# Attention loop: three PSUM banks taken by age for chunks, maxima and turns, P·V in one bank, and the score pair first in a unit

## The chip, the core and the metric

The kernel runs on one core of one Trainium2 chip. The metric is the device time of one execution in microseconds (us). Five engines run their own instruction streams and meet only at semaphores: TensorE (PE), VectorE (DVE), ScalarE (ACT), GpSimd (POOL) and SyncE (SP), which issues most of the DMAs. PE writes its products to PSUM, which has eight banks of 128 x 512 float32.

## What is computed

Attention over 4 batches of 1024 tokens with 16 heads of 16 channels, with a residual and layer norms, and then a layer of 8 experts of which each token takes 2. The softmax is taken over all keys, and the causal mask is applied afterwards without a new normalisation.

```
x = L0_attn_content                                   # 4 x 1024 x 256
x = x + _layernorm(attn(_layernorm(x), Wq, Wk, Wv))
x = x + _layernorm(ffn(_layernorm(x), router_w, w_fc, w_proj))
# attn
scores = einsum('bqhd,bkhd->bhqk', Q, K) / sqrt(HEAD_DIM)
alpha = softmax(scores); alpha = where(causal, alpha, 0)
Y = einsum('bhqk,bkhd->bqhd', alpha, V)
# ffn
topk_w, topk_idx = top_k(softmax(x @ router_w), 2)    # weights normalised
out = sum over e of combine[:, e] * (gelu(x @ w_fc[e]) @ w_proj[e])
```

## The kernel before

**Stages.** First the layer norm, Q, K and V of all tokens (up to about 150 us, already mixed with the first units of attention), then the attention loop (up to about 983 us), in whose last part the router and the first expert tile are worked in, and then 71 tiles of tokens through the experts. Only the attention loop is changed, with the two places where the experts begin.

**The loop.** The 64 pairs of batch and head are taken in 16 groups of four heads. A period is `U` = 32 units; period p works on the score pairs of group p, and on later steps of the groups before it. Every engine has its own `body`, which walks the same units in order. The order of steps inside a unit is as written there, and the unit of each step comes from the `at_...` lists: `due(at, k)` gives what stands in unit k, with how many periods back its group is. The steps of a group, counted in units from its first score pair:

- unit k, 0 to 31, **score pair**: two matmuls of 96 x 512 into banks 0 and 1 (k even) or 2 and 3 (k odd), line 1261. DVE reduces the 1024 scores of each query to a **maximum**, line 1699. Pair k waits until the maximum of k-2 is done.
- after every 8 units POOL splits the maxima into three bfloat16 parts (lines 731 to 737), PE transposes them (`at_m`, line 1274), ACT copies the result (line 905), and POOL spreads it into the last rows of the query operand (line 744).
- from unit 41, two **chunks** a unit, 64 in all: scores again, with the maximum taken off by the operand's last rows. Three of four are transposed scores (keys on partitions, line 1074), of which ACT takes the exponential into `et_sb` (line 921). The fourth, a corner (line 1067), is there for its row sum alone (line 916). The chunks go by turns to banks 4 and 5 (`ebank`), so a chunk waits for the exponential of the chunk two before; the last group has a ring of four.
- 12 **P·V bursts** (`pieces`, line 1104) at units 45, 48, 50, 53, 56, 58, 61, 64 for queries 512 to 1023 (bank 7), and 66, 69, 72, 74 for queries 0 to 511 (bank 6). A burst is 512 columns of float32 for four heads, each on its own 32 partitions; 8 of 12 have a diagonal part of 128 columns more, which waits for the mask product on POOL (line 765).
- `at_poc`, units 65 and 75: DVE **copies** the product out of its bank to `po_sb` (line 1710). `at_turn`, 67 and 77: PE **turns** it by four transposes back into the same bank (line 1248). `at_norm`, 69 and 79: DVE divides by the row sums (**norm**, lines 1720 to 1730). A burst on a bank's first key block waits for the norm of the group before.

The transposed maxima go to banks 6 and 7, rows 96 to 119, and wait for the norm there.

From period 6 on DVE and POOL also work on the layer norms of finished tokens (`steady`, `STEADY`, lines 1527 to 1558), in fixed units. In periods 16 and 17, the **tail**, no pairs are left, and the router's steps stand in their place.

**Order in a unit before.** PE: turn, P·V burst, first chunk, score pair, transpose of the maxima, second chunk. DVE: maximum reduction, layer norm step, copy, norm. ACT: copy of the maxima, then the exponentials.

## Time and profile before

| | |
|---|---|
| median of 3 executions | 1539.58 us (1539.1 to 1542.72) |
| profiled execution | 1539.73 us, of which its span is 1537.8 us |
| mean granted clock of PE in it | 0.983 of full speed |
| busy, share of the span | PE 92%, PE's weight loads 53%, DVE 60%, ACT 52%, POOL 40% |
| costliest group of DVE | line 1699, 512 maximum reductions, 607.2 us, 1217 ns each |
| costliest group of ACT | line 921, 768 exponentials, 436.1 us |
| attention loop on PE | chunks (lines 1067, 1074), pairs (1261) and bursts (1104) |

A matmul's row runs from its start to its modelled end and overlaps the next ones, so how long PE needs is read from start to start. "Idle before" names what an engine waited for. The window view gives busy times of each engine in a stretch.

### The profile page before, as it was taken

The page shows a single profiled execution, that of the slowest core. Times are in us where ns is not written, and L with a number is a line of the kernel's source. Part 1 is how long each engine was busy: PE and PEld are TensorE (multiplying, and loading weights), DVE is VectorE, ACT ScalarE, POOL GpSimd, SP SyncE. Part 2 cuts the span into 40 slices and gives each one's busy share as a digit, 9 for nine tenths or more (in the row PEclk, how much of TensorE's full clock was granted, in tenths as well). Part 3 has the DMA queues.
Part 4 walks back from the last instruction along what each step waited for, and adds up shares of the span by engine and source line. Part 5 has one row for each costly group of instructions (what it writes and reads, how often), then busy time and mean ns, then how long its engine had stood idle before and what let it go on. Part 6 is the DMA issues. An engine that isn't in the chain of part 4 may idle for free.

```text
span 1537.8 us, 28642 instructions
## 1 busy us (share of the span) xinstructions
PE 1417.4 (92%) x9774; PEld 820.1 (53%) x9775; DVE 925.1 (60%) x1740; ACT 805.4 (52%) x1717; POOL 610.9 (40%) x729
## 2 busy tenths in 40 slices
PE   6788999999999999999999998899999999999990
PEld 3444233333333233323332333699999999999980
DVE  4587787777888988898889887861111111111115
ACT  4444777777777777777777787321111111111114
POOL 2234334443454445444544441433333333333325
PEclk9999999999999999999999999999999999999995
DMA  3665732022202331223114141656666666666646
GB/s 122 155 158 126 247 42 42 7 37 42 42 15 28 42 42 18 25 42 42 20 23 97 56 138 57 175 163 192 172 178 191 176 178 187 182 175 182 189 113 222
DMA packets 100405, 166.85 MB, mean 108 GB/s; under 512 B 12400, under 2 KB 67568, under 8 KB 100304
## 3 DMA queue, kind: packets, MB, share of 16 engines
q1 hardware_dynamic: 86192, 146.08, 35.8%
q0 software_dynamic: 13632, 18.69, 7.6%
q10 hardware_dynamic: 480, 0.79, 0.3%
q8 instruction: 56, 0.92, 0.3%
q14 instruction: 45, 0.37, 0.1%
HBM read 130.76 MB, written 34.77 MB: 108 GB/s over the span
## 4 chain that ended last, share of the span: by engine, by line
PE 68%; DVE 18%; issue 6%; ACT 5%; POOL 2%; DMA 2%; ACTq 0%; POOLq 0%; DVEq 0%
PE ps L1206 16%; PE ps L1220 15%; PE ps L1104 11%; DVE negmax L1699 10%; PE ps L1074 9%; PE ps L1261 8%; ACT wfc L921 2%; PE ps L1043 2%; PE ps L1067 2%; POOL wfc L833 1%; PE ps L1248 1%; DVE x L1517 1%; PE ps L1193 1%; DVE mv L1506 1%; PE ps L1052 1%
## 5 line engine op out<-in xcount | busy, mean ns | idle before, releaser
L1699 DVE TENSOR_REDUCE negmax<-ps 128x1 f32<-128x1024 f32 x512 | 607.2, 1217 | 134.3 <-PE ps L1261 132.8
L921 ACT ACTIVATE wfc<-ps 128x512 f32<-128x512 f32 x768 | 436.1, 595 | 162.7 <-PE ps L1074 157.0
L976 ACT ACTIVATE wfc<-ps 128x512 f32<-128x512 f32 x142 | 84.8, 597 | 420.9 <-PE ps L1206 420.9
L1206 PEld LDWEIGHTS ps<-yx,wfc 128*128 128x128 f32 x2272 | 264.3, 192 | 4.2 <-issue 0.9
L1206 PE MATMUL ps<-yx,wfc 128*128 128x128 f32 x2272 | 265.7, 275 | 0.2 <-issue 0.2
L765 POOL TENSOR_TENSOR wfc<-wfc,causal 128x512 f32<-128x512 f32 x128 | 162.3, 1268 | 241.3 <-issue 108.8
L1220 PE MATMUL ps<-arena,wfc 128*128 x1136 | 257.3, 379 | 0.9 <-DMA arena<-in_L_ffn_w_proj 0.7
L821 POOL DMA_INDIRECT expert_out<-wfc,rt x71 | 113.0, 1592 | 299.9 <-DVE wfc L1663 291.9
L1220 PEld LDWEIGHTS ps<-arena,wfc 128*128 128x128 f32 x1136 | 210.3, 190 | 27.2 <-issue 1.6
L1261 PE MATMUL ps<-arena 96*128 96x512 bf16 x704 | 211.6, 382 | 9.1 <-DMA arena<-qk_parts 5.7
L1074 PE MATMUL ps<-arena 120*128 120x512 bf16 x528 | 202.0, 390 | 11.9 <-ACT wfc L921 0.4
L1104 PE MATMUL ps<-wfc 128*16 128x128 f32 (+4 forms) x2304 | 161.4, 381 | 0.1
L1663 DVE TENSOR_SCALAR wfc<-ps,rt 128x256 f32<-128x256 f32 x71 | 34.3, 483 | 203.1 <-PE ps L1220 203.1
L916 ACT ACTIVATE ps<-ps 128x512 f32<-128x512 f32 x256 | 149.6, 584 | 10.7 <-PE ps L1067 1.0
L1074 PEld LDWEIGHTS ps<-arena 120*128 120x128 bf16 x528 | 50.1, 96 | 183.9 <-ACT wfc L921 117.3
L1651 DVE SCALAR_TENSOR_TENSOR rt<-yx,rt 128x1 f32 (+1 forms) x71 | 15.5, 219 | 200.0 <-PE ps L1193 200.0
L1261 PEld LDWEIGHTS ps<-arena 96*128 96x128 bf16 x704 | 67.8, 99 | 63.1 <-issue 12.0
L1104 PEld LDWEIGHTS ps<-wfc 128*17 128x17 f32 (+1 forms) x2304 | 60.8, 97 | 75.2 <-issue 47.9
L1074 PE MATMUL ps<-wfc 120*128 120x512 bf16 x240 | 93.0, 388 | 6.4 <-ACT wfc L921 0.8
L1261 PE MATMUL ps<-wfc 96*128 96x512 bf16 x320 | 95.6, 379 | 0.3
L1104 PE MATMUL ps<-wfc,vone 128*17 128x128 f32 (+3 forms) x1024 | 94.6, 441 | 1.0
L744 POOL TENSOR_TENSOR arena<-mT,dmask 24x1024 bf16<-24x1024 bf16 x44 | 83.3, 1894 | 14.8 <-ACT mT L905 11.8
(208 smaller groups left out, 1259.3 us busy)
## 6 DMA issues: line engine op xcount, KB each, us to landing
wfc<-in_L_ffn_w_fc SPq DMA_DIRECT2D x71, 1024.0 KB, 5.3
arena<-qk_parts SPq DMA_DIRECT2D x126, 128.0 KB, 5.6
qk_parts<-x SPq DMA_DIRECT2D x32, 384.0 KB, 2.8
arena<-in_L_ffn_w_proj SPq DMA_DIRECT2D x8, 1024.0 KB, 8.3
wfc<-qk_parts SPq DMA_DIRECT2D x60, 128.0 KB, 5.8
expert_out<-rt SPq DMA_DIRECT2D x3, 1408.0 KB, 12.2
yx<-in_L_attn_content SPq DMA_DIRECT2D x8, 512.0 KB, 4.3
x<-in_L_attn_content SPq DMA_DIRECT2D x1, 4096.0 KB, 14.0
```

The lines of the kernel that those rows point to most:

```text
L744: pool.tensor_tensor(qs[(u - back) % NSL][MROW:MROW + MR, hl, :] .rearrange("p (i q) -> p i q", i=QT), mT[MROW:MROW + MR, :].unsqueeze(1). ...
L765: pool.tensor_tensor(md_sb[b % NET], et_sb[b % NET][:, :, q:q + P], causal[:, :].unsqueeze(1).to_broadcast([P, GH, P]), ALU.mult).then_inc ...
L821: pool.indirect_dma_start(out=ys_d, in_=yslot[t % 2], in_offset=None, out_offset=bass.IndirectOffsetOnAxis(ap=tok[:, t:t + 1], axis=0), co ...
L916: nc.scalar.activation(bk(ebank(c, g)), bk(ebank(c, g)), ACT.Exp, accum_out=den_u[:, (u - back) % NSL, hl, i:i + 1]).then_inc(s_expB, 1)
L921: nc.scalar.activation(et_sb[b % NET][:, hl, :], bk(ebank(c, g)), ACT.Exp).then_inc(s_expB, 1)
L976: nc.scalar.activation(hidT[s][:, 4 * hf:4 * hf + 4, :], bk(1 + hf).rearrange("p (c t) -> p c t", c=4), ACT.Gelu).then_inc(s_ge, 1)
L1074: nc.tensor.matmul(bk(ebank(c, g)), ks[v][0:MROW + MR, hl, i * P:(i + 1) * P], qs[v][0:MROW + MR, hl, hf * 512:(hf + 1) * 512], start=True ...
L1104: ins = nc.tensor.matmul(out[32 * hl:32 * hl + rows, q0:q1], lhs, rhs, start=(i == 0 and piece == 0 and n == 0), stop=False, skip_group_ch ...
L1206: ins = nc.tensor.matmul(bk(1 + hf)[:, c * P:(c + 1) * P], w1[s][:, kc * FF + (4 * hf + c) * P:kc * FF + (4 * hf + c + 1) * P], xsT[:, kc, :],
L1220: ins = nc.tensor.matmul(bk(5 + s)[:, 0:D], hidT[s][:, c, :], arena[:, ds(off + c * D, D)], start=(c == 0), stop=(c == FC - 1))
L1261: ins = nc.tensor.matmul(bk(2 * (k % 2) + hf), qs[u][0:SROWS, hl, i * P:(i + 1) * P], ks[u][0:SROWS, hl, hf * 512:(hf + 1) * 512], start=T ...
L1699: nc.vector.tensor_reduce(negmax[:, hl % 2, i:i + 1], ps[:, 2 * (k % 2):2 * (k % 2) + 2, :], AX.XY, ALU.max, negate=True).then_inc(s_max, 1)
```

## The change

Four things are changed, all in the attention loop.

1. **Banks.** Banks 4, 5 and 6 form one ring. A list of all its users in order (`ring_entries`: turns, chunks, maxima) is built, and each takes the bank whose last user is oldest (`ring_banks`). A turn's bank is not taken again by the next `HOLD` = 4 users. Each user waits for its bank's last one by name (`ring_free`): an exponential, a norm or a copy of maxima. The last group's ring of four goes. The first group's maxima stay in bank 7.
2. **P·V in bank 7 alone.** The first burst of each half waits for the copy of the half before it (`s_poc`), no longer for a norm.
3. **DVE.** Copy and norm stand ahead of the maximum reduction in their unit, and `at_norm` is two units earlier: the norm stands in the unit of its turn, 67 and 77.
4. **PE.** The score pair stands ahead of the burst and of both chunks.

In the tail the first tokens for the experts are transposed in bank 2 and no longer wait for a norm; the waits for the last exponential and the norm move from `first_half` and `transpose_x` to the first `second_half`.

```diff
-        at_norm = [x + 2 for x in at_turn]
+        at_norm = list(at_turn)
...
-        LAST_RING = (4, 5, 1, 2)
-
-        def ebank(c, g):
-
-            if isinstance(g, int) and g == NGR - 1:
-                return LAST_RING[c % 4]
-            return 4 + c % 2
...
+        def tx_bank(t):
+
+            return 2 if isinstance(t, int) and t == 0 else 7
...
+        def ring_entries():
+
+            out = []
+            for x in range(PRO, (NGR + 2) * U):
+                p, k = divmod(x, U)
+                out += [("turn", p - back, j) for j, back in due(at_turn, k) if live(p, back)]
+                chunks = [("chunk", p - back, c) for c, back in due(at_chunk, k) if live(p, back)]
+                out += chunks[:1]
+                out += [("maxima", p - back, hl) for hl, back in due(at_m, k) if live(p, back)]
+                out += chunks[1:]
+            return out
+
+        RING = ring_entries()
+        HOLD = 4
+
+        def ring_banks():
+
+            bank, user = {}, {}
+            last, held, until = {4: -3, 5: -2, 6: -1}, 0, -1
+            for n, x in enumerate(RING):
+                b = min((b for b in last if b != held or n > until), key=last.get)
+                bank[x], user[x] = b, RING[last[b]] if last[b] >= 0 else None
+                last[b] = n
+                if x[0] == "turn":
+                    held, until = b, n + HOLD
...
+            def ring_free(kind, g, x):
+                if RING_USER[kind, g, x] is None:
+                    return
+                last, g, x = RING_USER[kind, g, x]
+                if last == "chunk":
+                    pe.wait_ge(s_expB, NCH * g + x + 1)
+                elif last == "turn":
+                    pe.wait_ge(s_norm, 2 * g + x + 1)
+                else:
+                    pe.wait_ge(s_mtc, GH * g + x + 1)
+
             def chunk(p, u, c, back):
...
-                if isinstance(g, int) and g == NGR - 1 and c >= 2:
-                    pe.wait_ge(*((s_max, QT * NH) if c < 4 else (s_expB, NCH * g + c - 3)))
-                else:
-                    wait_pos(pe, s_expB, NCH * g + c - 1)
+                ring_free("chunk", g, c)
...
-                    et, out = et_sb[b % NET], bk(6 + hf)
+                    et, out = et_sb[b % NET], bk(7)
...
-                        wait_pos(pe, s_norm, 2 * (g - 1) + (j + 1))
-                        pe.wait_ge(s_mtc, min(GH * g + M_BEFORE_PV[j], NH) if isinstance(g, int) else
-                                   GH * g + M_BEFORE_PV[j])
+                        wait_pos(pe, s_poc, 2 * g + j)
...
             def first_half(t, s, hf):
-                if isinstance(t, int) and t == 0 and hf == 0:
-                    pe.wait_ge(s_expB, NCH * NGR)
...
                         pe.wait_ge(s_poc, 2 * (p - back) + (j + 1))
+                        ring_free("turn", p - back, j)
...
-                    pieces(p, u, k)
-                    todo = due(at_chunk, k)
-                    chunk(p, u, *todo[0])
                     if live(p, 0):
                         hl, i = divmod(k, QT)
...
                         ins.then_inc(s_S, 1)
+                    pieces(p, u, k)
+                    todo = due(at_chunk, k)
+                    chunk(p, u, *todo[0])
```

On DVE the blocks of the copy and of the norm move ahead of the block of the maximum reduction and of `steady`; ACT's exponentials only take the bank's new name.

The order on PE in units 65 to 67 of a later group, before: `s_expB` is the exponentials, `s_max` the maximum reductions, `s_sp` the split maxima, `s_poc` the copies. The first burst on queries 0 to 511 is the row with 17x128.

```order
L1261 MATMUL ps<-arena 128x512
L1274 MATMUL ps<-identb,mparts 24x128 [waits s_norm,s_sp]
L1074 MATMUL ps<-wfc 128x512 [waits s_expB]
L1104 MATMUL ps<-wfc,vone 17x128 [waits s_expB,s_mtc,s_norm]
...
L1261 MATMUL ps<-arena 128x512 [waits s_max]
L1261 MATMUL ps<-arena 128x512
L1067 MATMUL ps<-wfc 128x512 [waits s_expB]
L1248 MATMUL ps<-ident,wfc 128x128 [waits s_poc]
L1248 MATMUL ps<-ident,wfc 128x128 x3
L1074 MATMUL ps<-wfc 128x512 [waits s_expB]
L1261 MATMUL ps<-arena 128x512 [waits s_max]
```

And the same place now; line 1290 is the pair, 1107 and 1100 the chunks, 1135 the burst, 1304 the transpose of the maxima, 1280 the turn:

```order
L1304 MATMUL ps<-identb,mparts 24x128 [waits s_expB,s_sp]
L1107 MATMUL ps<-wfc 128x512 [waits s_expB]
L1290 MATMUL ps<-arena 128x512 [waits s_max]
L1290 MATMUL ps<-arena 128x512
L1135 MATMUL ps<-wfc,vone 17x128 [waits s_expB,s_poc]
...
L1107 MATMUL ps<-wfc 128x512 [waits s_expB]
L1100 MATMUL ps<-wfc 128x512 [waits s_mtc]
L1280 MATMUL ps<-ident,wfc 128x128 [waits s_expB,s_poc]
L1280 MATMUL ps<-ident,wfc 128x128 x3
L1290 MATMUL ps<-arena 128x512 [waits s_max]
L1290 MATMUL ps<-arena 128x512
```

The pair stands ahead of the burst and, after the turn, ahead of both chunks; the burst waits for the copy instead of norm and maxima, and the turn also waits for the bank of an older exponential.

DVE at the first copy and norm of a group, before (line 1710 is the copy, 1728 the norm's product, 1699 the maximum reduction):

```order
L1699 TENSOR_REDUCE negmax<-ps 128x1 [waits s_S]
L1710 COPY wfc<-ps 128x512 [waits s_T4,s_pv]
L1699 TENSOR_REDUCE negmax<-ps 128x1 [waits s_S] x4
L1723 RECIPROCAL rden<-ps 128x16 [waits s_T4]
L1728 TENSOR_TENSOR yx<-ps,rden 128x4x64 [waits s_rc]
L1699 TENSOR_REDUCE negmax<-ps 128x1 [waits s_S] x2
L1535 MEMSET pause 128x1 [waits s_norm]
```

And now (lines 1732, 1750 and 1758):

```order
L1758 TENSOR_REDUCE negmax<-ps 128x1 [waits s_sp,s_S]
L1732 COPY wfc<-ps 128x512 [waits s_T4,s_pv]
L1758 TENSOR_REDUCE negmax<-ps 128x1 [waits s_S] x2
L1745 RECIPROCAL rden<-ps 128x16 [waits s_T4]
L1750 TENSOR_TENSOR yx<-ps,rden 128x4x64 [waits s_rc]
L1758 TENSOR_REDUCE negmax<-ps 128x1 [waits s_S] x5
L1566 MEMSET pause 128x1 [waits s_norm]
```

The copy stands one reduction earlier, and between copy and norm are two reductions instead of four.

## Rows read from the trace of the kernel before

**Rows 1.** The page: busy us of each engine, its share, its instructions.

```profile
PE 1417.4 (92%) x9774; PEld 820.1 (53%) x9775; DVE 925.1 (60%) x1740; ACT 805.4 (52%) x1717; POOL 610.9 (40%) x729
```

**Rows 2.** Windows: busy us (instructions), clock, DMA; two periods and the tail.

```profile
345.16:395.41 50.25, 48.52 (x356) 16.07 (x348) 39.96 (x40) 38.54 (x85) 21.18 (x30) 1.00 0.22 32
395.41:446.38 50.97, 48.77 (x356) 16.14 (x348) 45.04 (x59) 38.55 (x85) 23.15 (x32) 1.00 0.22 32
...
900.90:966.00 65.10, 54.56 (x569) 25.62 (x568) 50.55 (x276) 49.59 (x121) 20.34 (x20) 0.97 0.38 119
```

**Rows 3.** Timeline of PE, two stretches between bursts: start us, us, engine, line, instruction.

```profile
705.34 0.41 PE L1104 MATMUL ps<-wfc,vone 128*17 128x256 f32 x4
...
706.77 0.60 PE L1261 MATMUL ps<-arena 96*128 96x512 bf16 x2
707.21 0.38 PE L1074 MATMUL ps<-arena 120*128 120x512 bf16 x1
707.62 0.39 PE L1074 MATMUL ps<-arena 120*128 120x512 bf16 x1
...
708.76 0.39 PE L1074 MATMUL ps<-arena 120*128 120x512 bf16 x1
...
709.77 0.52 PE L1104 MATMUL ps<-wfc,vone 128*17 128x384 f32 x4
...
713.29 0.62 PE L1104 MATMUL ps<-wfc,vone 128*17 128x512 f32 x4
```

**Rows 4.** Timeline of PE: pair starts around two bursts, and around a turn.

```profile
352.70 0.60 PE L1261 MATMUL ps<-wfc 96*128 96x512 bf16 x2
...
354.92 0.38 PE L1261 MATMUL ps<-wfc 96*128 96x512 bf16 x1
...
366.09 0.38 PE L1261 MATMUL ps<-wfc 96*128 96x512 bf16 x1
...
368.08 0.38 PE L1261 MATMUL ps<-wfc 96*128 96x512 bf16 x1
...
396.17 0.38 PE L1261 MATMUL ps<-arena 96*128 96x512 bf16 x1
...
396.82 0.38 PE L1248 MATMUL ps<-ident,wfc 128*128 128x128 f32 x2
...
397.48 0.38 PE L1261 MATMUL ps<-arena 96*128 96x512 bf16 x1
```

**Rows 5.** Waits of the whole trace: who waited for whom, us, times, longest.

```profile
PEld ps L1074 <- ACT wfc L921: 174.2, 368, 1.0
ACT wfc L921 <- PE ps L1074: 157.0, 204, 4.7
...
PEld ps L1248 <- DVE wfc L1710: 16.9, 14, 1.4
...
PEld ps L1104 <- POOL wfc L765: 9.9, 19, 0.8
```

**Rows 6.** Timeline of ACT behind the first burst of rows 3.

```profile
706.97 1.74 ACT L921 ACTIVATE wfc<-ps 128x512 f32<-128x512 f32 x3 [0.84 <-PE ps L1074]
...
709.29 1.18 ACT L921 ACTIVATE wfc<-ps 128x512 f32<-128x512 f32 x2
```

**Rows 7.** Timeline of PE and DVE: transpose of maxima, copy of the product, turn.

```profile
712.81 0.23 PE L1274 MATMUL ps<-identb,mparts 128*24 128x128 bf16 x1
...
717.54 0.38 PE L1067 MATMUL ps<-wfc 120*128 120x512 bf16 x1
...
718.09 0.68 DVE L1710 COPY wfc<-ps 128x512 f32<-128x512 f32 x1
...
718.82 0.44 PE L1248 MATMUL ps<-ident,wfc 128*128 128x128 f32 x2 [0.91 <-DVE wfc L1710]
```

**Rows 8.** Norm's product on DVE, and variance's last step (ns min/median/max).

```profile
708.83 0.42 DVE L1728 TENSOR_TENSOR yx<-ps,rden 128x256 f32<-128x256 f32 x1
...
L1506 DVE TENSOR_SCALAR mv<-mv x13: 169/1189/1399, 408.7 to 984.8; 128x2 f32<-128x2 f32 x10, 128x4 f32<-128x4 f32 x3
```

70 lines of the change are left out of this document (35 added, 35 removed).

## The prediction

> **What bounds the kernel now.** I read the page's busy shares first, then the periods, then one period instruction by instruction. The page says PE 92%, DVE 60%, ACT 52% [rows 1]. These are averages over two stages. From 983 us on the expert stage keeps PE full, and nothing in the change reaches into it. The attention loop, up to about 983 us, is the only place to win or lose.
>
> The loop repeats every 32 units, and the windows cut from one copy of a P·V half to the same copy of the next group of heads show it: 50.25 us without the layer norm work on DVE, 50.97 us with it, the same in every later group [rows 2]. DVE does 39.96 us in the first kind and 45.04 in the second, ACT 38.54 in both. So five more microseconds of DVE work cost 0.72 us: DVE is not what sets the period, ACT isn't either, and PE's 48.5 to 48.8 busy us contain latencies of matmuls that overlap waits. I therefore count PE by starts.
>
> **PE's own work in a period.** Where nothing is waited for, two pair matmuls of 512 columns take 0.44 us to the next start (706.77 to 707.21), 0.22 each [rows 3]. A unit of two chunks and two pair matmuls is thus 0.88. A P·V burst with a diagonal part adds 1.31: the unit from 352.70 to 354.92 is 2.22, less 0.88 and a wait of 0.02. One without adds 1.09: 366.09 to 368.08 is 1.99, by the same subtraction [rows 4]. A turn that waits for nothing adds 0.43: it starts at 396.82, three matmuls behind 396.17, and 396.17 to 397.48 is 1.31 [rows 4]. The transpose of the maxima adds 0.22 (an estimate from its own row, 0.23 long) [rows 7]. Per period: 32 x 0.88 = 28.2, 8 x 1.31 = 10.5, 4 x 1.09 = 4.4, 4 x 0.22 = 0.9, 2 x 0.43 = 0.9, together 44.8 us. PE stands still for 50.25 - 44.8 = 5.4 us in a period of the first kind and 6.2 in one of the second.
>
> **Where it stands still.** (a) Between bursts, for ACT. Behind pair 706.77 chunks start at 707.21 and 707.62, not 707.43: 0.19 lost. From 707.62 to the same place a unit on, 708.76, are 1.14, not 0.88: 0.26 lost [rows 3]. The ring has two banks, so a chunk waits for the exponential two before it, while ACT takes 0.5 to 0.6 us for each. The largest row of the waits table has 174 us of it over the loop, for the weight loads; part of that lies under running matmuls [rows 5]. By starts it is 0.2 to 0.3 in each of the 20 units without a burst, 4.5 us a period. Yet ACT then idles 0.84 us behind the burst [rows 6]. Both wait in turns: a buffer is missing, not speed. (b) At the turn. PE stands from 717.54 to 718.82 for the copy of the product, which sits on DVE behind a maximum reduction: 1.28 less 0.22 is 1.06; at 396.82 it was nil [rows 4, 7]. The table has 16.9 us for 14 such waits [rows 5], so about 1.0 a period. That is 5.5 together, and closes the sum.
>
> **The change, part by part.**
>
> *Ring of three, 64 chunks a period.* Walk three units without a second burst, burst start 705.34 to burst start 709.77, now 4.43 us [rows 3]. With three banks the chunk behind the burst, its partner and the next one find free banks (ACT is done with all of them during a burst of 1.3 us). The following chunk needs an exponential that started 0.4 us after its matmul's start and ends 0.5 later, by which time two pair matmuls have run. Only the last chunk of the three units waits, about 0.1. So 1.31 + 3 x 0.88 + 0.1 = 4.05, 0.38 less. For two units between bursts 1.31 + 1.76 = 3.07, where 709.77 to 713.29 is now 3.52, of which 0.22 is the maxima transpose: 0.22 less. A period has eight of the longer and four of the shorter kind: 3.0 + 0.9 = 3.9 us. ACT stays under its own limit: from 706.97 to 709.29 a corner and three exponentials take 2.32 for two units [rows 6], 37 a period and some 38 with the four copies of maxima, against 45.
>
> *Maxima and turns in the ring.* They take 6 of 70 entries, and a turn keeps its bank for four entries, so two units after each turn have two banks again. Bounds: nothing (a burst stands in both stretches) to 2 x 2 x 0.25 = 1.0 a period. I take 0.3, since before the later turn ACT is just caught up.
>
> *Copy and norm ahead of the maximum reduction.* The copy starts as soon as the burst before is done, and the turn two units on finds it done: 1.0 us a period saved. The copy (0.68 [rows 7]) and the norm (a product of 0.42 [rows 8] behind a reciprocal) were already on DVE, and no instruction is added. Queued behind them now is one reduction each, for which PE waits only two units later. The norm stands in the turn's own unit and can hold DVE for it: bounds 0 to 0.6, I take 0.2.
>
> *P·V in one bank.* Burst 8 now waits for the copy of bursts 0 to 7, which DVE does at unit 65 of the group while the burst is at 66. Burst end to copy end is 0.7 to 1.0 us. In between PE has two chunks, a pair, a chunk, the maxima, a chunk and a pair, 1.98 us by the prices above. So I take 0; if that cover were gone it would be 1.0. Burst 0 of the next group stands two units behind the other copy: 0. A rule speaks against this part. The Trainium skill (Perfetto Trace Analysis, Matmuls) wants independent matmul groups to rotate through different PSUM banks so that evacuation overlaps the next group. By it the two hand-overs of a period would each cost the copy and its signals, some 0.9 us, and the time would be the sum below plus about 26 us; the row of the turn shows the price, and the cover between the bursts is why I don't take it.
>
> *Pair first.* S P c c' in place of P c S c' is nearly a rotation: from pair to pair stand the same matmuls. It puts one pair (0.44) between a mask's maxima in POOL's queue and its burst. The waits of products on a mask are 19 and hold 9.9 us [rows 5], 0.6 a period. I take 0.2 a period of that.
>
> *Sum, first kind:* 3.9 + 1.0 + 0.2 - 0.3 - 0.2 = 4.6, less 0.2 for new small waits: 4.4, so 45.9 us, 1.1 above PE's own work. *Second kind:* DVE's 45.04 is now as large as PE's 44.8, and both are uneven. Units 3 to 13 hold the norm, two statistics, a variance whose last step takes 1.19 in the median and 1.40 at most, against 0.17 at the least [rows 8], and a copy: some 15.0 on DVE against 13.5 on PE; in the rest PE leads. With two pair buffers DVE can lag by about one reduction. Bounds 45.9 to 48.9; I take 47.0, 4.0 less.
>
> Periods: 4.75 of the first kind (153 to 395 us) and 10 of the second (395 to 901 us) [rows 2]. 4.75 x 4.4 = 20.9 and 10 x 4.0 = 40.0, 60.9 us.
>
> *Tail, 901 to 983 us.* The last group had a ring of four and now has three, with turns in it. ACT is busy 49.6 of 65.1 us there and DVE 50.6 [rows 2], PE waits for both in turn. The norm comes two units earlier, and the first expert product no longer waits for the last exponential. Bounds -3 to +4; I take +1.5. Prologue: 0.
>
> The profiled execution took 1539.73, 0.15 above the median. 1539.7 - 60.9 + 1.5 = 1480.3; I round to 1481.
>
> **The rivals.**
>
> *A: the gain is there in half.* DVE becomes the bound in ten periods. Its queue is strict, and copy, norm and layer norm stand in the wrong units. For it: 45.04 of DVE work already. Against it: 50.97 held the same work with 5.9 idle. Periods of 48.2 and 49.0: 4.75 x 2.0 + 10 x 2.0 = 29.5 less, 1512.
>
> *B: PE's own limit is reached in both kinds,* 44.9 and 45.4: 4.75 x 5.3 + 10 x 5.6 = 81 less, 1461. Against it is the unevenness above.
>
> *C: nothing changes.* Turns, maxima and the hold take away the third bank, so chunks still wait as with two: only the turn's wait goes and the waits for norm and mask take its place. 1537. Against it: only 8 of 64 chunks stand in a hold.
>
> *D: slower.* The hand-over in one bank is on the path, twice a period, with the norm ahead of a reduction that PE is waiting for: 2 x 0.9 + 2 x 0.75 = 3.3 a period in, 1.0 (turn) and a third of the ring's gain (1.3) out, 1.0 x 14.75 = 15 us more, 1555. It decides where the copy ends later than 0.4 us after the pair ahead of burst 8 has started.
>
> **How the numbers follow.** Forecast 1481 (1468 to 1497 by its own unknowns): 0.60. A 0.18, B 0.07, C 0.05, D 0.05; the skill's rule about banks, at 1480 + 26 = 1506, 0.05. A measurement of this kernel can tell 0.3%, 4.6 us, from no change. Faster 0.90, same 0.05, slower 0.05. Range 1465 to 1514: it takes in A's centre and the rule's time, and leaves out C, D and most of B.
>
> **What would show it.** Copies of the first half should stand 45.5 to 46.5 us apart before the layer norm work and 46.5 to 48 with it. The wait of the turn for the copy should be gone; ACT's waits for chunks should fall below half of 157 us. Waits of P·V on the copy should be nil: if they are above 0.3 us each, D's mechanism is there. If DVE's idle time in a later period is under 1 us, DVE is the bound. I am wrong if chunks still start 0.41 us apart between bursts, if the period with layer norm stays above 49, or if the tail grows by over 5 us.

## The result, and the profile after

The changed kernel takes 1529.71 us (median of four runs, 1528.81 to 1530.95) against 1539.72 (1539.1 to 1542.72): a ratio of 0.9932, interval 0.9914 to 0.9949. It is faster by 10 us, and the forecast was 58. The profiled execution has a span of 1529.0, against 1537.8. The page's line of busy times, to be read against [rows 1]:

```profile
PE 1398.4 (91%) x9774; PEld 822.2 (54%) x9775; DVE 943.3 (62%) x1740; ACT 772.5 (51%) x1717; POOL 611.4 (40%) x729
```

No instruction was added on PE, DVE, ACT or POOL. ACT's busy time is 32.9 us shorter although its 1717 instructions are not: they overlap each other more often. DVE's is 18.2 us longer with the same 1740 instructions, so something stretched them. That is the first hint.

Now the windows of the changed kernel, cut at the same copies as [rows 2]: a period without layer norm, one with it, and the last three stretches up to the last copy. The columns are those of [rows 2].

```profile
336.04:384.53 48.49, 46.86 (x350) 16.19 (x349) 40.50 (x41) 36.17 (x84) 21.51 (x29) 1.00 0.24 34
435.20:485.86 50.66, 47.30 (x350) 16.05 (x349) 46.67 (x59) 36.38 (x84) 22.88 (x31) 1.00 0.23 32
840.53:892.60 52.07, 48.21 (x355) 16.60 (x353) 47.83 (x69) 38.21 (x89) 24.27 (x33) 1.00 0.15 46
892.60:946.63 54.03, 45.70 (x455) 20.75 (x456) 40.96 (x241) 40.28 (x98) 13.04 (x11) 0.94 0.41 134
946.63:964.36 17.73, 12.53 (x143) 5.58 (x142) 12.86 (x61) 12.04 (x29) 8.31 (x7) 0.98 0.31 94
```

The kernel before has in the last three:

```profile
854.37:904.58 50.21, 48.04 (x352) 16.19 (x344) 44.96 (x69) 38.14 (x84) 22.19 (x31) 1.00 0.17 52
904.58:958.01 53.43, 43.78 (x453) 20.70 (x442) 41.54 (x241) 40.62 (x99) 12.85 (x11) 0.97 0.41 131
958.01:973.12 15.11, 12.09 (x143) 5.36 (x142) 12.45 (x62) 11.65 (x29) 8.43 (x7) 1.00 0.25 79
```

The periods without layer norm went from 50.25 to 48.49, 1.76 us less where 4.4 were forecast. Those with it went from 50.97 to 50.66, 0.3 less where 4.0 were. By the first of these late copies the changed kernel is 13.8 us ahead (854.37 less 840.53); 3.9 of that it already has at the first copy of all (190.57 against 194.45). The last three stretches take 123.83 us against 118.75, so 5.1 of that is given back. From the last copy to the end of the span both take 564.6 to 564.7: the expert stage did not change.

The waits table of the changed kernel (who waited for whom, us in total, times, longest), against [rows 5]:

```profile
ACT wfc L946 <- PE ps L1107: 210.7, 216, 5.1
...
PEld ps L1107 <- ACT wfc L946: 83.2, 203, 1.6
...
PEld ps L1280 <- DVE wfc L1732: 2.7, 10, 0.3
...
PEld ps L1135 <- DVE wfc L1732: 1.5, 2, 1.3
```

The wait of the turn for the copy is gone (16.9 us before, 2.7 now). PE's weight loads wait half as long for an exponential (174.2, now 83.2). P·V in one bank costs next to nothing (1.5). But ACT waits longer for chunks than before (157.0, now 210.7): exponentials are now short of chunks, and chunks still wait for exponentials. That is a question of order, not of the number of banks.

**Between bursts.** The timeline of PE, between two bursts, where nothing else stands in the way: three pair starts.

```profile
697.15 0.60 PE L1290 MATMUL ps<-arena 96*128 96x512 bf16 x2
...
698.01 0.59 PE L1290 MATMUL ps<-arena 96*128 96x512 bf16 x2
...
699.06 0.60 PE L1290 MATMUL ps<-arena 96*128 96x512 bf16 x2
```

Units of 0.86 and 1.05 us, where [rows 3] has 1.14: here the third bank does what the prediction said. A few units later, PE and ACT around a transpose of maxima:

```profile
701.03 0.38 PE L1100 MATMUL ps<-arena 120*128 120x512 bf16 x1
701.25 0.60 PE L1290 MATMUL ps<-arena 96*128 96x512 bf16 x2
701.68 0.38 PE L1107 MATMUL ps<-wfc 120*128 120x512 bf16 x1
701.99 0.23 PE L1304 MATMUL ps<-identb,mparts 128*24 128x128 bf16 x1
702.49 0.39 PE L1107 MATMUL ps<-wfc 120*128 120x512 bf16 x1 [0.27 <-ACT ps L941]
702.71 0.60 PE L1290 MATMUL ps<-arena 96*128 96x512 bf16 x2
```

```profile
701.24 0.60 ACT L946 ACTIVATE wfc<-ps 128x512 f32<-128x512 f32 x1 [0.96 <-PE ps L1107]
701.73 0.59 ACT L941 ACTIVATE ps<-ps 128x512 f32<-128x512 f32 x1
702.24 0.19 ACT L941 ACTIVATION_READ_ACCUMULATOR ps<-ps 128x1 f32 x1
```

The unit from 701.25 to 702.71 takes 1.46 us. The three banks hold a chunk, a corner and the maxima, and the next chunk can only start at 702.49, when ACT has let go of the corner (L941 with the read of its accumulator, until 702.43). ACT in its turn had idled 0.96 us behind the burst. A unit of two chunks, a pair and the maxima is 0.88 + 0.22 = 1.10 by the prediction's prices, so 0.36 are lost, four times a period: 1.4 us. In the period from 336 us on all four such units take 1.46.

**In the layer norm's periods.** DVE and POOL of the changed kernel, two places within one period, and an undisturbed copy of the second step:

```profile
703.25 1.89 POOL L768 TENSOR_TENSOR arena<-mT,dmask 24x1024 bf16<-24x1024 bf16 x1
...
703.31 1.86 DVE L1537 TENSOR_SCALAR mv<-mv 128x2 f32<-128x2 f32 x1
```

```profile
716.21 1.89 POOL L768 TENSOR_TENSOR arena<-mT,dmask 24x1024 bf16<-24x1024 bf16 x1 [1.27 <-ACT mT L929]
...
716.44 1.94 DVE L1548 SCALAR_TENSOR_TENSOR x<-yx,rstd,x 128x256 f32<-128x256 f32 x1
```

```profile
711.03 0.48 DVE L1548 SCALAR_TENSOR_TENSOR x<-yx,rstd,x 128x256 f32<-128x256 f32 x1
```

The variance's last step works on two numbers per partition and takes 1.86 us; it ends at 705.17, and POOL's product of 1.89 at 705.14. The same add takes 0.48 alone and 1.94 beside that product. Both DVE instructions began just behind POOL's, and both lasted until it was through (the add 0.28 us longer).

### The profile page after: what moved, and what is told of

It reads as the page before. It is cut to its first block, busy times and chain, and to the rows that moved or that the text cites. A ratio compares the mean times of both kernels' runs of the same rounds, so it can differ in the third digit from the quotient of the medians.

```text
span 1529.0 us, 28662 instructions
## 1 busy us (share of the span) xinstructions
PE 1398.4 (91%) x9774; PEld 822.2 (54%) x9775; DVE 943.3 (62%) x1740; ACT 772.5 (51%) x1717; POOL 611.4 (40%) x729
## 4 chain that ended last, share of the span: by engine, by line
PE 66%; DVE 19%; issue 6%; ACT 6%; POOL 2%; DMA 2%; ACTq 0%; POOLq 0%; DVEq 0%
PE ps L1235 16%; PE ps L1251 16%; DVE negmax L1758 12%; PE ps L1135 10%; PE ps L1290 8%; PE ps L1107 7%; PE ps L1068 2%; PE ps L1100 2%; ACT ps L941 2%; ACT wfc L946 2%; DVE x L1548 1%; POOL wfc L857 1%; PE ps L1224 1%; PE ps L1280 1%; PE ps L1077 1%
## 5 line engine op out<-in xcount | busy, mean ns | idle before, releaser
L946 ACT ACTIVATE wfc<-ps 128x512 f32<-128x512 f32 x768 | 423.3, 598 | 213.9 <-PE ps L1107 210.7
L1001 ACT ACTIVATE wfc<-ps 128x512 f32<-128x512 f32 x142 | 84.8, 597 | 422.1 <-PE ps L1235 390.5
L1107 PE MATMUL ps<-arena 120*128 120x512 bf16 x528 | 185.8, 387 | 12.7 <-ACT ps L941 10.6
L941 ACT ACTIVATE ps<-ps 128x512 f32<-128x512 f32 x256 | 153.6, 600 | 0.0
L1290 PEld LDWEIGHTS ps<-arena 96*128 96x128 bf16 x704 | 62.9, 99 | 99.0 <-DVE negmax L1758 34.8
L768 POOL TENSOR_TENSOR arena<-mT,dmask 24x1024 bf16<-24x1024 bf16 x44 | 83.3, 1893 | 18.4 <-ACT mT L929 16.1
L1107 PE MATMUL ps<-wfc 120*128 120x512 bf16 x240 | 83.9, 384 | 5.9 <-ACT ps L941 5.3
```

The source lines that it names most:

```text
L768: pool.tensor_tensor(qs[(u - back) % NSL][MROW:MROW + MR, hl, :] .rearrange("p (i q) -> p i q", i=QT), mT[MROW:MROW + MR, :].unsqueeze(1). ...
L941: nc.scalar.activation(bank, bank, ACT.Exp, accum_out=den_u[:, (u - back) % NSL, hl, i:i + 1]).then_inc(s_expB, 1)
L946: nc.scalar.activation(et_sb[b % NET][:, hl, :], bank, ACT.Exp).then_inc(s_expB, 1)
L1001: nc.scalar.activation(hidT[s][:, 4 * hf:4 * hf + 4, :], bk(1 + hf).rearrange("p (c t) -> p c t", c=4), ACT.Gelu).then_inc(s_ge, 1)
L1107: nc.tensor.matmul(bk(ring_bank("chunk", g, c)), ks[v][0:MROW + MR, hl, i * P:(i + 1) * P], qs[v][0:MROW + MR, hl, hf * 512:(hf + 1) * 512 ...
L1290: ins = nc.tensor.matmul(bk(2 * (k % 2) + hf), qs[u][0:SROWS, hl, i * P:(i + 1) * P], ks[u][0:SROWS, hl, hf * 512:(hf + 1) * 512], start=T ...
```

## The experiments

Two ideas stood against each other for where the 48.7 us between forecast and result went: the order within a unit (pair first, and the maxima between two chunks), and DVE as the bound in the layer norm's periods. For the second kind of period the two can hold together. All times are medians, with the ratio to the kernel before and its interval. A period is the distance of two copies of a first half; "first" is without layer norm, "second" with it.

### The parts of the change, one at a time

**Pair back between the chunks**, all else as changed. In PE's unit:

```
-                    if live(p, 0):          # the pair, ahead of pieces and chunks
...
                     pieces(p, u, k)
                     todo = due(at_chunk, k)
                     chunk(p, u, *todo[0])
+                    if live(p, 0):
...
```

> One part undone: the score pair stands again between the two chunks and behind the P.V burst; ring, one bank, copy and norm stay as changed. Theory R (ring users wait for ACT because PE issues two chunks back to back right behind a burst): with the pair between them each chunk's bank is asked for 0.44 us later, the maxima unit falls from 1.46 us by 0.3 to 0.4, and the period without layer norm from 48.49 to 46.8 to 47.3, the kernel to 1505 to 1515 us. Rival P (pair first is what feeds DVE, as the change's order suggests): periods grow by 0.5 to 1, kernel 1535 to 1545. If it is a mere rotation, 1528 to 1531.

Measured: 1508.13 us, 0.9798 (0.9781 to 0.9814); first 47.36, second 49.06. With the pair back in its old place the changed kernel is 21.6 us faster. The place costs 1.1 us a period of the first kind, 1.6 of the second, and 2.3 in the layer norm stretch that starts at the 840.53 copy. It is no clean undo, though. The next rows are PE and DVE of this kernel: the last matmuls before burst 8, and the copy that it waits for.

```profile
379.17 0.68 DVE L1732 COPY wfc<-ps 128x512 f32<-128x512 f32 x1
```

```profile
378.26 0.60 PE L1293 MATMUL ps<-arena 96*128 96x512 bf16 x2
...
379.91 0.41 PE L1135 MATMUL ps<-wfc,vone 128*17 128x128 f32 x8 [0.53 <-DVE wfc L1732]
...
381.34 0.60 PE L1293 MATMUL ps<-arena 96*128 96x512 bf16 x2
```

The unit takes 3.08 us, where it is 2.17 in the changed kernel: the hand-over of the one P·V bank now costs 0.9. In this one unit pair first pays, since it puts a pair between the two bursts; in the others it costs more than the 21.6 us show.

**A ring of two**, turns and maxima in a bank of their own:

```
-                b = min((b for b in last if b != held or n > until), key=last.get)
+                b = min(((4, 5) if x[0] == "chunk" else (6,)), key=last.get)
```

> The third bank is taken from the chunks: they go by turns to banks 4 and 5 as before, turns and maxima have bank 6 alone; all else as changed. It says what the ring of three is worth. If the third bank is what shortened units without a burst from 1.08 to 0.87 and 1.05 us, they go back to 1.1, while the chunk behind the maxima no longer shares a bank with them: period without layer norm 49.5 to 50.5, kernel 1538 to 1548 us. If maxima and turns in the ring eat up what the third bank gives, the period stays at 48.5 and the kernel at 1527 to 1532.

Measured: 1570.92 us, 1.0201 (1.0184 to 1.0218); first 51.96, second 52.82. With pair first the third bank is worth 51.96 - 48.49 = 3.5 us in a period of the first kind, net of what maxima and turns cost as its users, and 41 us in all. The prediction had 3.9 for the bank and 0.3 for those users, for the old order. The expected time was missed upwards, and this pointed at the pair's new place: with two banks the changed kernel is slower than the kernel before.

**The kernel before, with the pair first** and nothing else:

```
+                    if live(p, 0):          # the pair, ahead of pieces and chunks
...
                     pieces(p, u, k)
                     todo = due(at_chunk, k)
                     chunk(p, u, *todo[0])
-                    if live(p, 0):
...
```

> The kernel before with one part of the change alone: the score pair first in each unit, with the ring of two, two banks for P.V and maxima, copy and norm as before. If pair first is a rotation without a price, as the prediction had it, 1536 to 1540 us. If it puts two chunks back to back behind the burst and makes them wait for ACT (the pair between chunks gave 21 us back in the changed kernel), the units with a burst and behind one grow by 0.2 to 0.4: period without layer norm 52 to 54, kernel 1560 to 1590 us.

Measured: 1569.93 us, 1.0195 (1.0178 to 1.0212); first 52.00, second 53.19. It costs 30 us, 1.75 to 2.2 a period. PE and ACT of this kernel behind a burst:

```profile
361.22 0.39 PE L1074 MATMUL ps<-arena 120*128 120x512 bf16 x1
361.45 0.38 PE L1067 MATMUL ps<-arena 120*128 120x512 bf16 x1
```

```profile
361.65 0.60 ACT L921 ACTIVATE wfc<-ps 128x512 f32<-128x512 f32 x1 [1.37 <-PE ps L1074]
```

Before, ACT got one chunk behind a burst with the pair behind that, and the second chunk followed one pair later, when ACT had room. Now the pair of the unit stands ahead of the burst, and both chunks come together at its end: ACT has idled for 1.37 us (0.84 in [rows 6]) and then has two exponentials at once, while the next chunks need their banks. The units without a burst grow to 1.19, 1.35 and 1.46.

**The kernel before, with the copy ahead of the maximum reduction** and nothing else: on DVE the copy's block is moved ahead of the reduction's.

> The kernel before with one part of the change alone: DVE's copy of the product stands ahead of the maximum reduction of its unit; norm, banks, ring and PE's order as before. The prediction put this part at 1.0 us a period, from the turn's wait of 1.06 us (16.9 us over 14 waits): that gives 1523 to 1528 us. Rival: the wait is lost elsewhere, since the reduction that now stands behind the copy holds up the pair two units on: 1535 to 1541.

Measured: 1526.7 us, 0.9918 (0.9903 to 0.9934); first 49.52, second 49.86. It saves 12 to 13 us: 0.73 a period of the first kind and 1.11 of the second, for 1.0 forecast. This one move alone does more than the change as a whole.

**The norm one unit later**, in the changed kernel:

```
-        at_norm = list(at_turn)
+        at_norm = [x + 1 for x in at_turn]
```

> The changed kernel with the norm one unit behind its turn (units 68 and 78) and still ahead of the maximum reduction. In the changed kernel DVE stands 17.7 us in 15 waits for the turn that PE does in the same unit, 4.3 of it once in the tail. Theory N: these waits are on the path where DVE sets the pace: periods with layer norm fall from 50.67 to 49.7 to 50.2, the tail by 3 to 4 us, the kernel to 1515 to 1522 us. Rival: the waits are hidden, only the tail's counts or none does: periods the same within 0.1, kernel 1525 to 1530.

Measured: 1530.96 us, 0.9939 (0.9923 to 0.9956); first 48.47, second 50.65. In the periods nothing changes: the norm in the turn's own unit costs nothing there that shows. In the tail it does. The last stretch falls from 17.73 to 16.36, while the one before it grows from 54.03 to 54.83. From the last copy to the end it takes 567.7 us in place of 564.65, because PE, early at the second product of the experts, now waits for their weights to land:

```profile
969.59 5.40 PE L1251 MATMUL ps<-arena,wfc 128*128 x16 [3.73 <-DMA arena<-in_L_ffn_w_proj]
```

So an unchanged total hides what the norm's unit does in the tail; the section on the tail comes back to it.

### DVE and POOL

**Layer norm steps moved away from POOL's product**, in the changed kernel:

```
-        STEADY = {7: ("bn_y", 0), 8: ("bn_y", 1), 9: ("var_y", 0), 13: ("add", 0), 17: ("add", 1),
-                  18: ("bn_x", 0), 19: ("bn_x", 1), 20: ("var_x", 0), 24: ("scale", 0), 26: ("scale", 1)}
-        ROOT_Y, ROOT_X = 10, 21
+        STEADY = {7: ("bn_y", 0), 8: ("bn_y", 1), 11: ("var_y", 0), 14: ("add", 0), 15: ("add", 1),
+                  17: ("bn_x", 0), 18: ("bn_x", 1), 20: ("var_x", 0), 22: ("scale", 0), 28: ("scale", 1)}
+        ROOT_Y, ROOT_X = 12, 21
```

> Only the units of the layer norm steps are changed: variance from unit 9 to 11, adds from 13 and 17 to 14 and 15, statistics from 18, 19 to 17, 18, scales from 24, 26 to 22, 28, POOL's root from 10 to 12, so that they keep away from POOL's spreading product (units 10, 18, 26, 2). Theory S (DVE's variance step, 1.86 us against 0.17, and one add, 1.94 against 0.48, stand because POOL's product of 1.89 us runs at the same time): the two rows fall to 0.2 and 0.5, DVE's busy time in a period from 46.68 to 43.5 to 44.5, the period from 50.67 to 48.5 to 49.3, ten of them: kernel 1510 to 1517 us. Rival (DVE just has too many instructions there and the length of single ones is hidden): period above 50.2, kernel 1525 to 1530.

Measured: 1514.71 us, 0.9844 (0.9827 to 0.9860); first 48.47, second 49.33. The first kind did not move (48.49 before the edit) and the second lost 1.3, 15 us in all. The variance's last step over the whole trace (ns min/median/max), in the changed kernel and here:

```profile
L1537 DVE TENSOR_SCALAR mv<-mv x13: 170/1861/1861, 399.3 to 975.2; 128x2 f32<-128x2 f32 x10, 128x4 f32<-128x4 f32 x3
```

```profile
L1537 DVE TENSOR_SCALAR mv<-mv x13: 168/170/178, 400.4 to 958.6; 128x2 f32<-128x2 f32 x10, 128x4 f32<-128x4 f32 x3
```

The same instruction, 1861 ns and 170 in the median, by its place alone; the add's mean fell from 1208 to 476.

**The same in the kernel before**, with the same table:

> The kernel before with the layer norm steps in the units of e3 (variance 11, adds 14 and 15, scales 22 and 28), nothing else. DVE's variance step is 1.20 us there and one add 1.06. Theory S says that the stretched steps cost time only where DVE sets the pace: in the kernel before, where PE does, 0 to 4 us less, 1536 to 1541. If the shared time costs PE too, 1525 to 1530 as in the changed kernel.

Measured: 1541.55 us, 1.0014 (1.0005 to 1.0024); first 50.25, second 51.16. The same two steps, here as L1506 and L1517 in groups by line (busy us, mean ns):

```profile
L1517 DVE SCALAR_TENSOR_TENSOR x<-yx,rstd,x 128x256 f32<-128x256 f32 x2 | 0.9, 474 | 0.0
...
L1506 DVE TENSOR_SCALAR mv<-mv 128x2 f32<-128x2 f32 x1 | 0.2, 170 | 0.0
```

The steps are as short as above, and nothing is gained; the second kind even takes 0.2 us more. Before the change PE set the pace of these periods too, and DVE's stretched steps lay in its idle time. The collision is old. What the change did is to bring PE so near to DVE that it counts.

### The place of the maxima

**Maxima one unit later, behind the pair and ahead of a burst:**

```
-        LAG_M, LAG_E, LAG_B = 9, 10, 9
+        LAG_M, LAG_E, LAG_B = 10, 10, 9
...
-                out += chunks[:1]
                 out += [("maxima", p - back, hl) for hl, back in due(at_m, k) if live(p, back)]
-                out += chunks[1:]
+                out += chunks
```

and in PE's unit the transpose stands right behind the pair.

> The transpose of the maxima is moved from between the two chunks of units 9, 17, 25, 1 to behind the pair and ahead of the burst of units 10, 18, 26, 2; its copy on ACT then falls into the burst, where ACT idles 1.0 to 1.25 us. Theory R: the second chunk of the old unit no longer waits for the corner's exponential, unit 1.46 back to 0.9 to 1.1, the new one grows by 0.2 to 0.3: period without layer norm 47.0 to 47.5, with it 50.0 to 50.6, kernel 1515 to 1524 us. Rival (the wait only moves on to the next chunk): 48.3 to 48.6 and 1527 to 1531.

Measured: 1493.38 us, 0.9704 (0.9687 to 0.9720); first 46.24, second 47.43. This is 36 us under the changed kernel, more than either theory gave. PE of this kernel: a pair, the maxima (the burst and two chunks follow), and the next two pairs.

```profile
346.50 0.60 PE L1289 MATMUL ps<-wfc 96*128 96x512 bf16 x2
347.02 0.23 PE L1300 MATMUL ps<-identb,mparts 128*24 128x128 bf16 x1
...
348.70 0.60 PE L1289 MATMUL ps<-wfc 96*128 96x512 bf16 x2
...
349.57 0.59 PE L1289 MATMUL ps<-wfc 96*128 96x512 bf16 x2
```

The burst's unit takes 2.20 us with the maxima in it, 2.17 without, and the unit that was 1.46 is 0.87. So the four transposes had cost 0.59 each between the chunks and cost 0.03 to 0.06 here: about 2.2 a period, and 48.49 - 46.24 = 2.25. They are users of the ring in both kernels; it is their place in it that costs. The second kind lost 3.2, because a later transpose also moves POOL's product, away from two of the DVE steps that it had stretched; their groups by line in this kernel:

```profile
L1554 DVE TENSOR_SCALAR yx<-x,mv,rstd 128x256 f32<-128x256 f32 x2 | 2.1, 1060 | 0.0
L1547 DVE SCALAR_TENSOR_TENSOR x<-yx,rstd,x 128x256 f32<-128x256 f32 x2 | 1.0, 476 | 0.0
```

The adds are back at 476 ns. One of the two scale steps, 1060 in the mean, now collides.

**That scale step two units later as well:**

```
-                  18: ("bn_x", 0), 19: ("bn_x", 1), 20: ("var_x", 0), 24: ("scale", 0), 26: ("scale", 1)}
+                  18: ("bn_x", 0), 19: ("bn_x", 1), 20: ("var_x", 0), 24: ("scale", 0), 28: ("scale", 1)}
```

> The kernel with the maxima under the burst (1493.4 us), and the second scale step of the layer norm moved from unit 26 to 28. There the first of the two scale steps or the second runs beside POOL's spreading product: their mean is 1.06 us against 0.41 in the runs that moved it. Theory S: DVE's busy time falls by 1.3 a period, the period with layer norm from 47.43 to 46.5 to 46.9, kernel 1484 to 1489 us. Rival, DVE's queue has slack at that place: 47.4 and 1492 to 1494.

Measured: 1485.53 us, 0.9650 (0.9634 to 0.9667); first 46.24, second 46.63. The second kind loses another 0.8, by one number in a table.

**Maxima under the burst, layer norm steps moved, and the pair between the chunks:** the pair moved as in the first diff above, the table as in the diff on the layer norm steps, and the maxima as in the one just shown, here ahead of the burst and of both chunks.

> Three edits together: maxima transposed under the burst, pair between the chunks, layer norm steps moved off POOL's spreading product. The single gains were 36, 22 and 15 us against 1529.7. If they are apart, 1460 us; but PE's own work is 44.8 us a period, so no period can be under it: with periods of 45.0 to 45.8 without and 45.8 to 46.8 with layer norm 1472 to 1482. If the pair in the middle and the maxima under the burst mend the same wait, 1484 to 1490.

Measured: 1507.54 us, 0.9787 (0.9771 to 0.9804); first 46.72, second 48.37. I had this one down as the best of all. With the maxima out of the way the pair between the chunks is worse than pair first (46.72 against 46.24), because the hand-over of the P·V bank is then on the path: its unit is 3.08 us as above, 0.9 more, and the other units together are 0.4 shorter. In the second kind that explains 0.5 of the 1.7 us over the scale step's kernel; none of the layer norm steps is stretched here, and what makes up the rest is open. Three gains of 15 to 36 us, measured one at a time, did not add up.

### The rest of the ring

**Hold of two in place of four**, on top of the scale step's kernel:

```
-        HOLD = 4
+        HOLD = 2
```

> As e9 with HOLD = 2: a turn's bank may be taken again after two users instead of four, with a wait for the norm. If the hold, not the norm, makes the units behind a turn long (1.02, 1.19 and 1.35 us in e4), they fall by 0.1 to 0.3 and the kernel by 3 to 8 us against e9. If the norm is late, because DVE does it up to two units after PE's turn, the chunk waits for it and the pair behind it is late: 5 to 20 us more.

Measured: **1481.56 us, 0.9625 (0.9608 to 0.9643), the fastest of all**; first 45.85, second 46.28. Two of its windows:

```profile
331.63:377.48 45.85, 45.49 (x350) 16.04 (x349) 39.94 (x41) 35.51 (x84) 21.58 (x29) 1.00 0.26 36
655.19:701.48 46.29, 45.81 (x350) 16.00 (x349) 42.93 (x60) 35.50 (x84) 22.97 (x31) 1.00 0.25 35
```

Two units behind the turns shrink, from 1.35 to 0.87 and from 1.19 to 1.08, and one grows from 0.87 to 1.05: 0.4 a period. DVE does 42.93 us in the second kind, 3.7 less than in the changed kernel, with one instruction more in the window.

**The turn behind the pair**, and the norm a unit later, on top of the scale step's kernel (hold of four): the block of the turn moves behind the pair's, and `at_norm` is `at_turn` + 1.

> As e9, and the turn behind its unit's score pair instead of ahead of it, with the norm one unit later. In e4 the turn waits 0.36 us for the exponential of its ring bank in the unit of 1.89 us, and the unit two behind it is 1.35 instead of 0.87 long because two banks are left. If the wait for the bank is what the turn costs, the pair's 0.44 covers it: 0.3 to 0.5 a period less, 4 to 8 us less than e9. If the hold costs it, nothing changes, within 2 us of e9.

Measured: 1483.04 us, 0.9632 (0.9616 to 0.9649); first 45.87, second 46.40. It saves 2.5 us, less than expected: 0.37 and 0.23 a period. Here too PE waits for the weights of the experts behind the last copy, 2.87 us.

**Both of these together:**

> Maxima under the burst, second scale step in unit 28, turn behind the pair with the norm one unit later, HOLD 2. e10 and e12 each gained 2.5 and 4 us on e9 (1485.5). If turn and hold are the same wait 1480 to 1483 us; if they are two, 1477 to 1480.

Measured: 1495.06 us, 0.9712 (0.9698 to 0.9725); first 45.94, second 46.89. A miss: slower than either alone. PE in the unit behind a turn, with the DVE instruction it waits for:

```profile
665.19 0.39 PE L1106 MATMUL ps<-arena 120*128 120x512 bf16 x1 [0.48 <-DVE yx L1749]
```

```profile
664.70 0.42 DVE L1749 TENSOR_TENSOR yx<-ps,rden 128x256 f32<-128x256 f32 x1
```

With the short hold the ring gives the turn's bank to a chunk before the norm, now a unit later, has read it. The longer hold had hidden that. The unit takes 1.52 us, 1.19 with the longer hold. In the tail the stretch up to the last first half grows to 58.6 us (56.7 with the short hold alone, 54.0 in the changed kernel), and behind the last copy it takes 3.1 us more than with the short hold alone.

### The tail

**A ring of four in the last group** as it was before, on top of the kernel with the maxima under the burst: bank 1 joins at the last group's chunks, and the first expert product waits for the last exponential again, as it did before.

```
+                if x[0] == "chunk" and x[1] == NGR - 1 and x[2] == 2:
+                    last[1] = -4
```

> The kernel of the maxima under the burst (1493.4 us) with a fourth bank (bank 1) for the chunks of the last group, as the kernel before had there. In the changed kernel the stretch from the copy of the last but one group's first half to the last copy took 5.1 us more than before. Theory: the smaller ring of the last group costs part of it: 1489 to 1491 us. Rival: the norm in the turn's unit alone does it: 1492 to 1494.

Measured: 1493.07 us, 0.9697 (0.9681 to 0.9713), against 1493.38 without it. The stretch up to the last first half is 54.02 in both, the last one 17.12 and 17.10. Bank and wait together, the fourth bank that the last group lost is not the reason.

**The first expert product three units later**, in the changed kernel, so that DVE's queue would not stand behind it:

```
-        ... AT_FIRST = 25, 29, 29, 31, 34, 39, 40, (43, 44)
+        ... AT_FIRST = 25, 29, 29, 31, 34, 39, 40, (46, 47)
```

> The changed kernel with one edit in the tail: the first expert product (32 matmuls, 3.8 us) stands in units 46 and 47 of the tail instead of 43 and 44, behind the last turn (unit 45). In the changed kernel DVE stands 4.3 us at the last norm, which waits for that turn, and from the copy of the last but one group to the last copy it takes 5.1 us more than before. Theory: DVE waits for a turn that is queued behind the product: that wait goes, kernel 1525.5 to 1528. Rival: the product's own place is what the tail needs: 1529 to 1534.

Measured: 1532.68 us, 0.9955 (0.9940 to 0.9970). What it was to shorten is this wait, the longest of DVE behind a turn, as the changed kernel has it on PE and on DVE:

```profile
950.11 0.66 PE L1280 MATMUL ps<-ident,wfc 128*128 128x128 f32 x4
```

```profile
951.61 0.26 DVE L1745 RECIPROCAL rden<-ps 128x16 f32<-128x16 f32 x1 [4.29 <-PE ps L1280]
```

It is still there, 4.29 us long, at 950.90, and it had to be. This is the turn of the last group's first half, in unit 35 of the tail, and the product stands in units 43 and 44. The edit moved something that this wait never stood behind.

**What the traces say of the last stretch.** The norm now stands in the turn's unit, so on DVE's strict queue a step of the router, which needs nothing of the turn, stands behind it. That step and PE's later wait for the result, first in the changed kernel:

```profile
952.24 0.27 DVE L1479 TENSOR_TENSOR rt<-rt,ps 128x32 f32<-128x32 f32 x2
```

```profile
962.38 0.19 PE L1186 MATMUL ps<-oh_bf,lower 128*128 128x32 bf16 x1 [3.64 <-DVE oh_bf L1468]
```

And in the kernel before, where the norm came two units later:

```profile
960.75 0.29 DVE L1448 TENSOR_TENSOR rt<-rt,ps 128x32 f32<-128x32 f32 x2 [2.05 <-PE ps L1158]
```

```profile
971.14 0.19 PE L1155 MATMUL ps<-oh_bf,lower 128*128 128x32 bf16 x1 [2.18 <-DVE oh_bf L1437]
```

The step began 2.74 us behind the copy and now begins 5.61 behind it, 2.87 later, and the stretch is 2.6 us longer. With the norm one unit later the wait for the turn is gone from DVE:

```profile
949.47 0.29 DVE L1479 TENSOR_TENSOR rt<-rt,ps 128x32 f32<-128x32 f32 x2 [2.32 <-PE ps L1189]
```

That is 3.00 us behind the copy, and the stretch is 16.36 in place of 17.73.

## Why the prediction was wrong

What was right, by its own steps:

- *PE's own work and the two waits.* 44.8 us of PE's own work a period. The fastest kernel reaches 45.85.
- *Ring of three:* 3.9 forecast less 0.3 for its other users, 3.5 net measured, though in the new order of PE.
- *Copy ahead of the reduction:* 1.0 forecast, 0.73 and 1.11 measured, and the wait of the turn is gone.
- *P·V in one bank:* 0 forecast, and the burst waits 1.5 us in the whole trace. The cover is the condition, as the prediction said: with one pair less between the bursts it waits 0.53 and the unit takes 0.9 more. The Trainium skill's rule (Perfetto Trace Analysis, Matmuls), that independent groups rotate through different banks, has its price of 0.9 there; in the changed kernel, which breaks it, the trace shows the 1.5 us.
- *Norm, in the periods:* 0.2 forecast, nothing that shows measured. The masks' waits, from which pair first was to gain 0.2, fell from 9.9 us to 2.5.

What failed, in order of size:

**1. Maxima in the ring, 0.3 taken and at most 1.0.** The bound was worked out for turns alone, as two units after each turn with two banks again, and for them it holds: the hold of two gave 0.4. The four maxima had only their own 0.22 each. But an entry that stands between two chunks puts the second of these behind a bank that ACT holds with a corner's exponential and the read of its accumulator. It costs 0.59 a time, 0.22 of it foreseen, and moving the transposes ahead of a burst gave 2.25 a period of the first kind.

**2. Pair first, "nearly a rotation", taken as a gain of 0.2.** From pair to pair the same matmuls do stand in a unit, but not from burst to chunk to chunk. Alone it costs 30 us in the kernel before. In the changed kernel the pair between the chunks is 21.6 us faster, although the hand-over then costs 0.9 a period. The prediction walked the chunks behind a burst under "ring of three" with the order P c S c' of [rows 3], and never walked the new order. With the maxima moved, the same pair first is the better order, so its price belongs to the two together.

**3. DVE in the layer norm's periods.** The prediction had 45.04 of DVE work and saw its unevenness, with bounds up to 48.9; the period came out at 50.66, beyond them. What it read as an uneven step (169/1189/1399 ns in [rows 8]) was another engine's instruction on top of it. DVE steps that take 0.17 and 0.48 us alone take 1.86 and 1.94 beside POOL's product, and the change of PE's order moved them onto it: with pair first alone in the kernel before they already take 1.86 and 1.96, where that kernel has 1.19 and 1.06. DVE's 45.04 grew to 46.67. The prediction's sign for DVE as the bound, less than 1 us idle in a period, did not come: DVE has 4.0 us idle (50.66 - 46.67), and its stretched steps cost 1.3 us all the same, since they stand where PE waits. Moving the steps gave 1.34 a period and 15 us in the changed kernel, and nothing in the kernel before. The Trainium skill (SBUF — State Buffer, Who interferes with whom) says that VectorE and GpSimd share a pair of ports under an exclusive lock, held by whoever issues first for its whole instruction, and it counts a VectorE instruction with two inputs in SBUF among those that contend. The trace agrees: the add reads `yx` and `x`, begins 0.23 us behind POOL's product and takes 1.94 in place of 0.48. The variance's last step has one input, which this sentence does not cover; that it is held as well is shown by the runs alone. The row [rows 8] was there to be asked about, and this is the question that I left out.

**4. The tail, +1.5 taken, up to +4.** It was 5.1. The failed step is "the norm comes two units earlier", which stood there without a cost: 2.6 of the 5.1 lie in the last stretch, where the norm waits 4.29 us for its turn with the router's step behind it. Another 1.9 lie in the stretch from 840.53, 1.3 of them DVE's stretched steps (52.07; 50.74 with the steps moved). The last 0.6 are in the stretch from 892.60, where the granted clock was 0.94 against 0.97: it was 0.50, the lower level of 1.2 GHz, for 6.8 us from 936.34 on, and for 3.4 us from 949.50 in the kernel before. Half of full speed for 3.4 us more is worth up to 1.7 us (an estimate from the clock's rows). In the 10 us ahead of the fall PE was busy for 7.7 us in the changed kernel and for 6.2 in the kernel before.

The rivals: 1529.7 lies between A (1512) and C (1537) and outside the range. A had periods of 48.2 and 49.0. The first comes near the measured 48.49, but not by A's mechanism, since moving DVE's steps left that kind where it was; the second is 1.7 short of 50.66. C had the better mechanism for the first kind: turns, maxima and the hold take from the third bank (2.25 for the maxima's place, 0.4 for the hold). It had them take all of the ring's gain, of which 3.5 us a period are left. The prediction named what would refute it, and most of that came: 50.66 with layer norm ("above 49"), a tail of over 5, and ACT's waits for chunks at 210.7 instead of under 78.

The gap closes with the mended versions: maxima under the burst -36.3, scale step -7.9, hold of two -4.0, together 48.2 of the 48.7 us between forecast and result. The periods are then 45.85 and 46.28 where the forecast had 45.9 and 47.0, and the time is 1481.6 where it had 1481. That this hits the number is partly luck: the fastest kernel's last three stretches take 47.70 + 56.71 + 17.05 = 121.5 us, 2.7 more than before where 1.5 were forecast, and its second periods are 0.7 shorter than forecast.

Open: how exactly the 2.6 us of the last stretch divide. It takes 16.3 to 18.4 us in all versions of the changed kernel, and 15.1 to 16.2 in those of the kernel before, so part of the difference can lie in things other than the norm. In the profiled executions the first copy stands between 188.1 and 198.7 us. It is 190.57 in the changed kernel and 188.12 with only later steps moved, which is the same program up to there, so 2.45 us of it are the execution and not the kernel. The granted clock shows most of that: it was 0.50 for 6.8 us from 62.5 on in the one, and for 3.4 us from 63.4 on in the other, up to 1.7 us of PE's time (an estimate from these rows).

## What to carry to other kernels

A reorder within a loop that counts the same instructions from one mark to the next is not free: walk the new order from the longest block that feeds nobody (here the burst) to the first and second user of the ring behind it. A rarely used entry that joins a ring of buffers needs a place of its own, best where the engine that releases the ring is idle anyway. A step that waits in a strict queue delays what stands behind it, so moving it earlier can cost more than it gives. Before an edit makes a second engine the near bound, look through its instructions for those whose longest is several times their shortest: here another engine's instruction ran on top of them, and the cost only waited for its cover to go.

## What the runs showed of the hardware

- A DVE instruction of 0.17 us (128x2, fp32) takes 1.86 us beside one POOL instruction of 1.89 (24x1024, bf16), to within 0.03 us of its end. In the profile this is no idle time and no wait: it is busy time of DVE. Only the spread of one instruction's durations shows it.
- A transpose of 0.23 us costs 0.59 in the ring between two chunks and 0.03 to 0.06 in front of a burst of fp32 matmuls, less than its own length.
- An exponential with a sum holds its bank until the sum is read, 0.19 us more in a row of its own (702.24 behind 701.73), and the next user of the bank waits for that.
